# Issuing a chunk's four output blocks in one run on TensorE, with the side work of their positions behind them

## The chip, the cores and the metric

The kernel runs on one core of one Trainium2 chip. The metric is the device time of the whole program in microseconds (us), the median of several runs. The core's engines are named as in the profile: PE is TensorE, which multiplies matrices (PEld is its weight load), DVE is VectorE, ACT is ScalarE, POOL is GpSimd, and SP is the engine whose queue issues the DMAs here.

## The reference, cut to what matters

The input is x of shape (32, 128, 56, 56): 32 images of 128 channels and 3136 pixels ("tokens"). A first stage adds a binarised 3x3 convolution with batch normalisation to x. The second stage treats each pixel as a token of 128 numbers:

```python
t = t + ffn(_ln_t(t))
# inside ffn, for each image x (3136 tokens of 128), H = 512, k = 3136/2, kk = k - 1:
weights = (jnp.einsum('bsd,do->bso', x, wr) + br)[..., 0]      # router
_, idx = jax.lax.top_k(weights, k); sel_idx = idx[:, :kk]
h = jax.nn.gelu(jnp.einsum('bkd,dh->bkh', sel, w1) + b1)       # hidden blocks
y = jnp.einsum('bkh,hd->bkd', h, w2) + b2                      # output blocks
y = y * w_sel[..., None]                                       # gate
processed = zeros.at[batch_idx, sel_idx].set(y); return processed + x
```

The kernel computes h and y for all tokens and multiplies y by a gate that is the router's weight for chosen tokens and zero for the others.

## The kernel before, in words

Phase 1 (the convolution, about the first 530 us) is not touched. Phase 2 is one program for each engine, written out by hand, with semaphores between them. It handles an image in 7 chunks of 448 tokens, and a chunk in 8 positions, so an image has 56 positions (POS). The body `phase2(n, b)` runs over them in order; `c, j = divmod(pos, 8)`.

- At j 0 to 3 PE computes hidden block j of chunk c (three f16 matmuls, L939 to L941) into PSUM bank j; ACT drains it through GELU into `hs` (L495).
- At j 4 to 7 PE computes output block j - 4 of the chunk before (L950, f32, two matmul records for a block). The four blocks accumulate into one PSUM bank, which ACT drains into `yo` (L505, at j 7).
- After the block of a position comes its side work: steps of other images and stages, which tables of positions place (`TRANSPOSE_AT`, `NORM_AT`, and so on; a position from 56 on is in the next image's body). `due` looks up what is due at a position.

The side steps that this document speaks of:

- Token statistics of image n+1: PE transposes a chunk (L885; T0 to T6 at positions 1, 3, 4, 5, 9, 10, 11) into bank BC0 (even chunks) or BC1 (odd), and DVE takes statistics from it (`tile_stats`, L647). From the third on, a transpose waits until DVE has taken the one before the last. DVE turns them into mean and reciprocal deviation (POOL helps, then L670 on DVE), PE transposes these (`rows_of_stats`, L904, position 23), DVE splits them (the last step is L679), and SP copies them into rows with six DMAs (L369).
- Normalisation: `spread_stats` (positions 31, 39, 47, 54, then 7, 15, 20 of the next body) spreads these rows over the partitions, L917 into BC0 and L920 into BC1; DVE multiplies (u, L685) and subtracts (t, L694). L917 waits until transposes' statistics are taken. L920 waits until the gate before it has been used, since both live in BC1.
- Gate: `spread_gates` (positions 19, 24, 29, 33, 38, 45, 52; L930) spreads a chunk's gates into BC1, and DVE multiplies (`apply_gate`, L781).
- Search for the top k: DVE counts (L722), PE sums the counts (`sum_counts`, L959; positions 35, 39, 42, 46, 50, 53, then 2, 5), DVE chooses (L728). Then PE does `transpose_ties` (position 10), `scan_ties` (L972, position 13), and DVE makes the gates from it (L767 to L775); SP copies them to rows with three DMAs. Router matmuls (L895) stand at 15, 16, 17, 20, 21, 23, 27.

DVE walks through the positions in the same order with its own share of these steps, so each engine answers the other in turn. Bodies -1 to 2 and 29 to 32 are written out, bodies 3 to 28 are a hardware loop with two bodies a turn.

Of the kernel before, what the change touches and what calls it, by code (L numbers as in the profile page):

```python
# [21 lines left out]
NCH = TOK // T  # L22
# [6 lines left out]
NB = HID // C  # L29
# [48 lines left out]
def block_kernel(nc, consts, x_in, cw_in, cb_in, gamma_in, beta_in, wr_in, br_in, w1_in, b1_in,  # L78
# [12 lines left out]
    with ExitStack() as ctx:  # L91
# [167 lines left out]
        def wait_count(eng, semaphore, value):  # L259

            if not (isinstance(value, int) and value <= 0):
                eng.wait_ge(semaphore, value)
# [12 lines left out]
        def is_int(n):  # L275
            return isinstance(n, int)

        def has(n, low=0, high=n_img):

            return not is_int(n) or low <= n < high  # L280
# [6 lines left out]
        def due(table, shift, n, b, pos):  # L287

            steps = [table] if is_int(table) else table
            found = []  # L290
            for at, m, mb in ((pos, n + shift, (b + shift) % 2), (pos + POS, n + shift - 1, (b + shift + 1) % 2)):
                if at in steps and has(m):
                    found.append((m, mb, steps.index(at)))
            return found
# [533 lines left out]
        def _(pe):  # L828
# [46 lines left out]
            def transposes(m, b, c, n, pos):  # L875
                pe.wait_ge(x1_ready, m * NCH + c + 1)

                wait_count(pe, t_ready if c % 2 else u_ready, done(NORM_AT, 1, n, pos))
                if c % 2:
                    wait_count(pe, gated, done(OUT_AT, -1, n, pos))  # L880
                if c > 1:
                    pe.wait_ge(stats_taken, m * NCH + c - 1)
                for i in range(TPG):
                    lo = c * T + i * TILE
                    last = nc.tensor.transpose(ps[0:TILE, BC0 + c % 2, i * C:(i + 1) * C], xb[b][:, lo:lo + TILE], ident)  # L885
                last.then_inc(transposed, 1)

            def router(n, b, c):

                pe.wait_ge(tl_ready, n * NCH + c + 1)  # L890
                if c == 0 and has(n - 1):
                    pe.wait_ge(mask_step, (n - 1) * MASK_STEPS + 3)
                bank = ps[:, T_BANK, 0:T]
                for i, (w, t) in enumerate(((wsel_h, th), (wsel_h, tl), (wsel_l, th))):
                    last = M(bank, w[:, C - c:2 * C - c], cut(t, c), start=c == 0 and i == 0,  # L895
                             stop=c == NCH - 1 and i == 2)
                if c == NCH - 1:
                    last.then_inc(w_done, 1)

            def rows_of_stats(m, n, pos):  # L900
                pe.wait_ge(mr_ready, m + 1)
                wait_count(pe, u_ready, done(NORM_AT, 1, n, pos))
                for q in range(2):
                    last = nc.tensor.transpose(ps[0:NT, BC0, q * C:q * C + TILE], rm[:, q, :],  # L904
                                               ident[0:TILE, 0:TILE])
                last.then_inc(stat_rows, 1)

            def spread_stats(m, b, c, n, pos):

                g = m * NCH + c  # L910
                if c == 0:
                    pe.wait_ge(norm_rows_in, (m + 1) * 2 * PIECES * 16)

                wait_count(pe, u_ready, g)
                wait_count(pe, stats_taken, done(TRANSPOSE_AT, 1, n, pos + 1))
                wait_count(pe, rms_ready, done(STAT_AT, 1, n, pos + 1))
                M(ps[:, BC0, 0:T], ones_b[0:PIECES, :], cut(rows[0:PIECES, :], c), start=True, stop=True).then_inc(bc_stats, 1)  # L917
                wait_count(pe, t_ready, g)
                wait_count(pe, gated, done(OUT_AT, -1, n, pos + 1))
                M(ps[:, BC1, 0:T], ones_b[32:32 + PIECES, :], cut(rows[32:32 + PIECES, :], c), start=True, stop=True).then_inc(bc_stats, 1)  # L920

            def spread_gates(m, b, c, n, pos):
                g = m * NCH + c
                if c == 0:
                    pe.wait_ge(gate_rows_in, (m + 1) * PIECES * 16)

                wait_count(pe, gated, g)
                wait_count(pe, t_ready, done(NORM_AT, 1, n, pos))
                wait_count(pe, stats_taken, done(TRANSPOSE_AT, 1, n, pos + 1))
                M(ps[:, BC1, 0:T], ones_b[64:64 + PIECES, :], cut(rows[64:64 + PIECES, :], c), start=True, stop=True).then_inc(bc_gate, 1)  # L930

            def hidden(n, b, c, j):
                g = n * NCH + c
                if j == 0:
                    pe.wait_ge(tl_ready, g + 1)
                wait_count(pe, h_ready, (g - 1) * NB + j + 1)
                bank = ps[:, H_BANK + j, 0:T]
                blk = slice(j * C, (j + 1) * C)
                M(bank, w1_h[:, blk], cut(th, c), start=True, stop=False)  # L939
                M(bank, w1_h[:, blk], cut(tl, c), start=False, stop=False)  # L940
                M(bank, w1_l[:, blk], cut(th, c), start=False, stop=True).then_inc(h_done, 1)  # L941

            def output(n, b, c, j):
                g = n * NCH + c
                if j == 0:
                    wait_count(pe, y_taken, g)
                first, final = j == 0, j == NB - 1
                bank = ps[:, Y_BANK, 0:T]
                pe.wait_ge(h_ready, g * NB + j + 1)
                last = M(bank, w2_c[:, j, :], hs[(b + c) % 2][:, j, :], start=first, stop=final)  # L950
                if j == NB - 1:
                    last.then_inc(y_done, 1)

            def sum_counts(n, r):

                pe.wait_ge(part_counts, n * ROUNDS + r + 1)
                if r == 0:
                    pe.wait_ge(w_taken, n + 1)
                M(cnt_ps, cnt_c[:, :].to_broadcast([C, C]), cand_sel[:, :], start=True,  # L959
                  stop=True).then_inc(counts_summed, 1)  # L960

            def transpose_ties(n):
                pe.wait_ge(ties_ready, n + 1)
                R = slice(0, MR_ROWS)
                nc.tensor.transpose(ps[0:MR_COLS, T_BANK, 0:MR_ROWS], ties_sb, ident[R, R])
                M(off_ps, kt[R, K_ONES:K_ONES + MR_ROWS], rowg_c[R, :], start=True, stop=False)
                M(off_ps, kt[R, K_STRI:K_STRI + MR_ROWS], rowe_c[R, :], start=False, stop=True).then_inc(ties_t, 1)

            def scan_ties(n):

                pe.wait_ge(ties_copied, n + 1)
                M(ps[0:MR_ROWS, T_BANK, C:C + MR_COLS], et[:, :], kt[0:MR_COLS, K_TRIU:K_TRIU + MR_COLS],  # L972
                  start=True, stop=True).then_inc(ties_scanned, 1)

            def phase2(n, b):
                for pos in range(POS):
                    c, j = divmod(pos, 2 * NB)

                    if j < NB and has(n):
                        hidden(n, b, c, j)  # L980
                    if j >= NB and c > 0 and has(n):
                        output(n, b, c - 1, j - NB)
                    if j >= NB and c == 0 and has(n - 1):
                        output(n - 1, 1 - b, NCH - 1, j - NB)

                    at = (n, b, pos)
                    for m, mb, c in due(TRANSPOSE_AT, 1, *at):
                        transposes(m, mb, c, n, pos)
                    for m, mb, c in due(ROUTER_AT, 0, *at):
                        router(m, mb, c)  # L990
                    for m, mb, r in due(COUNT_AT, 0, *at):
                        sum_counts(m, r)
                    for m, mb, _ in due(MASK_AT, 0, *at):
                        transpose_ties(m)
                    for m, mb, _ in due(SCAN_AT, 0, *at):
                        scan_ties(m)
                    for m, mb, _ in due(STAT_AT, 1, *at):
                        rows_of_stats(m, n, pos)
                    for m, mb, c in due(OUT_AT, -1, *at):
                        spread_gates(m, mb, c, n, pos)  # L1000
                    for m, mb, c in due(NORM_AT, 1, *at):
                        spread_stats(m, mb, c, n, pos)

            pairs(pe, phase2, *P2, -1, n_img + 1)


# [20 lines left out]
```

## Time and profile before

| | before |
|---|---|
| time, median of 3 runs | 2380.06 us (2378.2 to 2380.43) |
| time of the profiled execution | 2379.78 us |
| its span | 2377.8 us |
| mean granted TensorE clock | 0.981 of 2.4 GHz |
| PE busy | 2202.0 us, 93% |
| DVE busy | 1622.5 us, 68% |
| ACT busy | 1222.9 us, 51% |
| POOL busy | 918.5 us, 39% |
| output matmuls L950 | 1792 records, 806.9 us, 564 ns each |

The busy shares are of the span. A matmul record overlaps the next one, so the step from one start to the next says more about PE than a record's length.

### The profile page before, as it was taken

To read this page: it belongs to the slowest core of one execution; us is meant where nothing else is said; L and a number is where in the kernel's file an instruction comes from. 1 tells how busy PE (TensorE), PEld (TensorE's weight loads), DVE (VectorE), ACT (ScalarE), POOL (GpSimd) and SP (SyncE) were. 2 spreads that over 40 slices of the span, in tenths; PEclk is the share of its full clock that TensorE was granted. 3 is DMA by queue.
4 is the path that set the end of the run, shared out by engine and by line. 5 is a ranking of instruction groups with operands and counts; after the bars stand their busy time and mean duration, and the time that the engine had idled before them with its cause. 6 is when DMAs were issued, how large, how long until landed. Compare 5 with 4: busy or idle time off the path is not lost. (4 is left out here: it accounts for less than half of the span.)

```text
span 2377.8 us, 38759 instructions
## 1 busy us (share of the span) xinstructions
PE 2202.0 (93%) x9739; PEld 1071.6 (45%) x9739; DVE 1622.5 (68%) x4887; ACT 1222.9 (51%) x2030; POOL 918.5 (39%) x714
## 2 busy tenths in 40 slices
PE   6999999966999999999999999998999999999997
PEld 3555555533444444444444444444444444444443
DVE  6777777755677766767676666666667676767764
ACT  4444444434555555555555555555555555555553
POOL 1000000024455544445445555454544454554433
PEclk9999999987999999999999999999999999999998
DMA  3444444431122222222222222222222222222201
GB/s 146 163 162 162 162 162 162 162 122 46 62 73 73 74 81 76 81 85 75 73 73 73 73 73 72 73 73 73 81 82 91 73 73 73 73 73 84 73 33 59
DMA packets 66710, 216.99 MB, mean 91 GB/s; under 512 B 28496, under 2 KB 33328, under 8 KB 62640
## 3 DMA queue, kind: packets, MB, share of 16 engines
q1 hardware_dynamic: 66464, 215.71, 25.1%
q14 instruction: 84, 0.69, 0.1%
q8 instruction: 18, 0.29, 0.1%
q10 hardware_dynamic: 144, 0.30, 0.0%
HBM read 136.70 MB, written 77.47 MB: 90 GB/s over the span
## 5 line engine op out<-in xcount | busy, mean ns | idle before, releaser
L950 PE MATMUL ps<-hs,w_c 128*128 128x448 f32 x1792 | 806.9, 564 | 0.8 <-ACT yo L505 0.6
L495 ACT ACTIVATE hs<-ps,b1c,undo 128x448 f32<-128x448 f32 x896 | 602.6, 718 | 136.6 <-PE ps L941 136.0
L412 POOL TENSOR_TENSOR tl<-tr,th 128x448 f16<-128x448 f32 x224 | 245.5, 1096 | 515.7 <-ACT th L518 393.9
L854 PE MATMUL ps<-yo,cwT 128*128 128x448 bf16 x2016 | 425.6, 356 | 0.0
L950 PEld LDWEIGHTS ps<-hs,w_c 128*128 128x128 f32 x1792 | 305.3, 192 | 191.7 <-issue 152.3
L505 ACT ACTIVATE yo<-ps,cols 128x448 f32<-128x448 f32 x224 | 141.9, 633 | 453.6 <-PE ps L950 453.6
L407 POOL TENSOR_TENSOR xb<-xb,zr 128x448 f32<-128x448 f32 x224 | 259.1, 1159 | 182.7 <-ACT zr L511 181.8
L419 POOL TENSOR_TENSOR yo<-yo,base 128x448 f32<-128x448 f32 x224 | 264.5, 1181 | 167.4 <-DVE yo L781 166.6
L939 PE MATMUL ps<-th,w_h 128*128 128x448 f16 x896 | 321.4, 359 | 0.0
L941 PE MATMUL ps<-th,w_l 128*128 128x448 f16 x896 | 319.3, 356 | 0.0
L940 PE MATMUL ps<-tl,w_h 128*128 128x448 f16 x896 | 319.2, 356 | 0.0
L854 PEld LDWEIGHTS ps<-yo,cwT 128*128 128x128 bf16 x2016 | 179.2, 98 | 196.2 <-issue 48.7
L476 ACT ACTIVATE y<-ps 128x448 f16<-128x448 f32 x224 | 121.9, 544 | 263.2 <-PE ps L854 263.2
L781 DVE TENSOR_TENSOR yo<-yo,ps 128x448 f32<-128x448 f32 x224 | 138.6, 619 | 152.4 <-PE ps L930 150.7
L647 DVE BATCH_NORM_STATS2 st<-ps 112x6 f32<-112x128 f32 x896 | 192.7, 282 | 62.9 <-PE ps L885 60.5
L511 ACT ACTIVATE zr<-y,bn_t,bn_s 128x448 f32<-128x448 f16 x224 | 168.8, 754 | 122.2 <-DMA y<-y_int 109.6
L685 DVE TENSOR_TENSOR ur<-xb,ps 128x448 f32<-128x448 f32 x224 | 138.5, 618 | 134.8 <-PE ps L917 76.5
L571 DVE BATCH_NORM_STATS2 base<-y 128x448 f16 (+1 forms) x224 | 140.5, 627 | 130.2 <-ACT y L476 130.2
L518 ACT ACTIVATE th<-tr 128x448 f16<-128x448 f32 x224 | 129.3, 577 | 139.8 <-DVE tr L694 127.6
L426 POOL TENSOR_TENSOR rm<-stw,kt 112x28 f32<-112x28 f32 x32 | 153.6, 4799 | 78.8 <-DVE stw L665 78.8
L885 PE MATMUL ps<-kt,xb 128*112 128x128 f32 x896 | 140.4, 281 | 41.7 <-DVE st L647 28.8
L403 POOL TENSOR_TENSOR sm<-sm,kt 128x1 f32<-128x1 f32 x1 | 0.6, 566 | 459.7 <-DVE sm L635 459.7
(131 smaller groups left out, 2709.7 us busy)
## 6 DMA issues: line engine op xcount, KB each, us to landing
xb<-x SPq DMA_DIRECT2D x31, 1568.0 KB, 7.6
xb<-x SPq DMA_DIRECT2D x33, 896.0 KB, 4.7
result<-yo SPq DMA_DIRECT2D x32, 896.0 KB, 4.4
y_int<-y SPq DMA_DIRECT2D x32, 784.0 KB, 3.7
xb<-x SPq DMA_DIRECT2D x33, 672.0 KB, 4.3
result<-yo SPq DMA_DIRECT2D x32, 672.0 KB, 3.4
y<-y_int SPq DMA_DIRECT2D x32, 448.0 KB, 5.3
y<-y_int SPq DMA_DIRECT2D x32, 336.0 KB, 4.8
```

The source lines that it names most:

```text
L407: nc.gpsimd.tensor_tensor(cut(xb[b], c), cut(xb[b], c), zr[(b + c) % 2][:, :], ALU.add).then_inc(x1_ready, 1)
L412: nc.gpsimd.tensor_tensor(cut(tl, c), tr[(b + c) % 2][:, :], cut(th, c), ALU.subtract).then_inc(tl_ready, 1)
L419: nc.gpsimd.tensor_tensor(cut(yo[b], c), cut(yo[b], c), cut(base[b], c), ALU.add).then_inc(out_ready, 1)
L426: nc.gpsimd.tensor_tensor(rm[:, 0, :], stw[:, 5, :], kt[0:TILE, K_MHALF:K_END], ALU.pow).then_inc(rstd_ready, 1)
L495: nc.scalar.activation(hs[(b + slot) % 2][:, j, :], ps[:, H_BANK + j, 0:T], ACT.Gelu_apprx_tanh, bias=b1c[:, j:j + 1], scale=undo[:, 1:2]) ...
L511: nc.scalar.activation(zr[(mb + c) % 2][:, :], cut(y16[mb], c), ACT.Relu, bias=bn_t[:, :], scale=bn_s[:, :]).then_inc(relu_ready, 1)
L647: last = V.bn_stats(st[:, c * TPG + i, :], ps[0:TILE, BC0 + c % 2, i * C:(i + 1) * C])
L854: last = M(bank, cwT[:, t, :], sg[b][:, c * ROWS + dy:c * ROWS + dy + ROWS, dx:dx + SIDE], start=t == 0, stop=t == TAPS - 1)
L939: M(bank, w1_h[:, blk], cut(th, c), start=True, stop=False)
L940: M(bank, w1_h[:, blk], cut(tl, c), start=False, stop=False)
L941: M(bank, w1_l[:, blk], cut(th, c), start=False, stop=True).then_inc(h_done, 1)
L950: last = M(bank, w2_c[:, j, :], hs[(b + c) % 2][:, j, :], start=first, stop=final)
```

## The change

PE's `phase2` no longer issues output block j - 4 at each of the positions j 4 to 7. At j 4 it issues all four, and then the side work of that position; j 5, 6 and 7 hold side work alone. No other engine's program changes, and no instruction is added or removed.

```diff
                     if j < NB and has(n):
                         hidden(n, b, c, j)
-                    if j >= NB and c > 0 and has(n):
-                        output(n, b, c - 1, j - NB)
-                    if j >= NB and c == 0 and has(n - 1):
-                        output(n - 1, 1 - b, NCH - 1, j - NB)
+                    for k in range(NB if j == NB else 0):
+                        if c > 0 and has(n):
+                            output(n, b, c - 1, k)
+                        if c == 0 and has(n - 1):
+                            output(n - 1, 1 - b, NCH - 1, k)
```

On PE, positions 3 to 7 of a body read before the change as follows. L885 are the transposes, L950 an output block, L959 the sum of counts, L917 and L920 the statistics spread at position 7.

```order
L885 MATMUL ps<-kt,xb 112x128 x4
L950 MATMUL ps<-hs,w_c 128x448
L885 MATMUL ps<-kt,xb 112x128 x4
L950 MATMUL ps<-hs,w_c 128x448
L885 MATMUL ps<-kt,xb 112x128 x4
L959 MATMUL ps<-cand_sel,cnt_c 128x15
L950 MATMUL ps<-hs,w_c 128x448 x2
L917 MATMUL ps<-rows,ones_b 128x448
L920 MATMUL ps<-rows,ones_b 128x448
```

The same place after the change:

```order
L885 MATMUL ps<-kt,xb 112x128 x4
L950 MATMUL ps<-hs,w_c 128x448 x4
L885 MATMUL ps<-kt,xb 112x128 x8
L959 MATMUL ps<-cand_sel,cnt_c 128x15
L917 MATMUL ps<-rows,ones_b 128x448
L920 MATMUL ps<-rows,ones_b 128x448
```

Transposes T2 and T3 now follow each other, and nothing stands between them, the sum and L917.

On PE, positions 35 to 39 (L930 is the gate spread of position 38) before:

```order
L959 MATMUL ps<-cand_sel,cnt_c 128x15
L950 MATMUL ps<-hs,w_c 128x448 x3
L930 MATMUL ps<-rows,ones_b 128x448
L950 MATMUL ps<-hs,w_c 128x448
L959 MATMUL ps<-cand_sel,cnt_c 128x15
L917 MATMUL ps<-rows,ones_b 128x448
L920 MATMUL ps<-rows,ones_b 128x448
```

and after:

```order
L959 MATMUL ps<-cand_sel,cnt_c 128x15
L950 MATMUL ps<-hs,w_c 128x448 x4
L930 MATMUL ps<-rows,ones_b 128x448
L959 MATMUL ps<-cand_sel,cnt_c 128x15
L917 MATMUL ps<-rows,ones_b 128x448
L920 MATMUL ps<-rows,ones_b 128x448
```

The output block that stood between L930 and L920 now stands ahead of L930. Positions 45 to 47 and 52 to 54 change in the same way. At positions 12 to 15 the scan L972, which stood after two of four output blocks, now stands after all four, directly ahead of the router matmuls L895:

```order
L950 MATMUL ps<-hs,w_c 128x448 x4
L972 MATMUL ps<-kt,et 98x32
L895 MATMUL ps<-th,wsel_h 128x448
L895 MATMUL ps<-tl,wsel_h 128x448
L895 MATMUL ps<-th,wsel_l 128x448
L917 MATMUL ps<-rows,ones_b 128x448
L920 MATMUL ps<-rows,ones_b 128x448
```

## Rows read from the trace of the kernel before

**Rows 1.** Timeline, positions 12 to 19: start us, us, engine, line, operation [idle before]
```profile
1697.71 1.67 PE L950 MATMUL ps<-hs,w_c 128*128 128x448 f32 x4
...
1699.31 0.35 PE L972 MATMUL ps<-kt,et 32*98 32x32 f32 x2
...
1699.70 0.25 DVE L767 TENSOR_SCALAR mk<-ps,srch 98x32 f32<-98x32 f32 x1 [0.28 <-PE ps L972]
...
1705.86 0.34 PE L930 MATMUL ps<-rows,ones_b 3*128 3x448 bf16 x1
```

**Rows 2.** Timeline of the same image, positions 20 to 23
```profile
1707.65 0.36 PE L917 MATMUL ps<-rows,ones_b 3*128 3x448 bf16 x1
...
1709.29 0.49 DVE L670 SCALAR_TENSOR_TENSOR rm<-stw,rm 112x28 f32<-112x28 f32 x1
...
1711.44 0.36 PE L904 MATMUL ps<-kt,rm 112*28 112x112 f32 x2
```

**Rows 3.** Timeline of the image before, positions 23 to 31
```profile
1656.22 0.36 PE L904 MATMUL ps<-kt,rm 112*28 112x112 f32 x2
...
1664.42 0.36 PE L917 MATMUL ps<-rows,ones_b 3*128 3x448 bf16 x1 [1.11 <-DMA rows<-rms]
```

**Rows 4.** Timeline, positions 36 to 39
```profile
1669.04 2.49 PE L950 MATMUL ps<-hs,w_c 128*128 128x448 f32 x6
1671.47 0.36 PE L930 MATMUL ps<-rows,ones_b 3*128 3x448 bf16 x1
...
1672.72 0.36 PE L920 MATMUL ps<-rows,ones_b 3*128 3x448 bf16 x1
```

**Rows 5.** Timeline of DVE beside them
```profile
1671.86 0.62 DVE L781 TENSOR_TENSOR yo<-yo,ps 128x448 f32<-128x448 f32 x1 [0.93 <-PE ps L930]
```

**Rows 6.** Timeline, positions 44 to 47
```profile
1675.55 1.68 PE L950 MATMUL ps<-hs,w_c 128*128 128x448 f32 x4
...
1679.26 0.36 PE L920 MATMUL ps<-rows,ones_b 3*128 3x448 bf16 x1
```

**Rows 7.** Timeline, position 52 to position 4 of the next body, no loop turn
```profile
1681.86 0.92 PE L950 MATMUL ps<-hs,w_c 128*128 128x448 f32 x2
...
1682.71 0.36 PE L930 MATMUL ps<-rows,ones_b 3*128 3x448 bf16 x1
...
1685.49 0.61 DVE L685 TENSOR_TENSOR ur<-xb,ps 128x448 f32<-128x448 f32 x1
...
1687.09 0.60 PE L885 MATMUL ps<-kt,xb 128*112 128x128 f32 x4
...
1687.73 0.89 DVE L647 BATCH_NORM_STATS2 st<-ps 112x6 f32<-112x128 f32 x4 [0.56 <-PE ps L885]
...
1689.13 0.92 PE L950 MATMUL ps<-hs,w_c 128*128 128x448 f32 x2
```

**Rows 8.** Timeline, positions 4 to 9 of that body
```profile
1692.08 0.89 DVE L647 BATCH_NORM_STATS2 st<-ps 112x6 f32<-112x128 f32 x4
...
1693.45 0.36 PE L917 MATMUL ps<-rows,ones_b 3*128 3x448 bf16 x1
...
1694.08 0.61 DVE L685 TENSOR_TENSOR ur<-xb,ps 128x448 f32<-128x448 f32 x1
...
1694.89 0.60 PE L885 MATMUL ps<-kt,xb 128*112 128x128 f32 x4
```

**Rows 9.** Timeline, positions 1 to 9 of a body that follows a loop turn
```profile
1632.24 0.89 DVE L647 BATCH_NORM_STATS2 st<-ps 112x6 f32<-112x128 f32 x4 [3.27 <-PE ps L885]
...
1638.81 0.61 DVE L685 TENSOR_TENSOR ur<-xb,ps 128x448 f32<-128x448 f32 x1
...
1639.52 0.60 PE L885 MATMUL ps<-kt,xb 128*112 128x128 f32 x4
```

**Rows 10.** Timeline of PE after another loop turn, position 5
```profile
1521.58 1.07 PE L885 MATMUL ps<-kt,xb 128*112 128x128 f32 x4 [1.26 <-DVE st L647]
```

**Rows 11.** That stretch: busy PE, PEld, DVE, ACT, POOL; granted clock; DMA share, GB/s
```profile
1521.00:1523.00 2.00, 1.42 (x6) 1.39 (x7) 1.50 (x10) 0.00 (x0) 0.00 (x0) 0.59 0.80 240
```

## The prediction

> **What bounds the kernel now.** I read the busy shares first (PE 93%), then the waits, and then the timeline of two images on all engines, row by row, because a reordering can only be priced at the places where one engine waits for another. The reader is to see in the rows how PE and DVE answer each other in turn. PE is nearly always the later of the two: it has work left when DVE's answer comes. Its few waits are short: 1.11 us at position 31 for the six DMAs of the statistics rows [rows 3], and after a loop turn two waits for DVE, the second 1.26 us [rows 10]. DVE starts a loop turn 3.27 us late [rows 9]; the row names PE, but T0 was done long before, so this is the turn of DVE's own program. What makes PE's waits so short is the output block, 0.75 us long (two blocks take 1.60 us up to the next side step [rows 1] and one takes 0.85 [rows 7]), that lies between a question to DVE and the next PE step that needs the answer. The change takes these blocks out from between.
>
> **The change, part by part.** Nothing is added or removed, so every cost is a wait. Times are offsets within one image. The delay from a DVE end to the PE start it releases is 0.1 us: u ends at 1639.42 and T4 starts at 1639.52 [rows 9]. I use it throughout.
>
> A. Positions 12 to 19. The scan L972 starts 1.60 us after the first output block [rows 1]; with four blocks ahead of it, 1.60 + 2 x 0.75 = 3.10, so 1.50 later. DVE builds the gates from it (L767 starts 0.39 after L972), SP copies them to rows, and L930 at position 19 needs them: 1705.86 - 1699.70 = 6.16 us after L767 [rows 1]. Between lie three DMAs that SP issues behind the gates, and no work that could be pulled closer. The row of L930 shows no wait, so PE and the rows come at about the same time today; I take it that L930 moves by the whole 1.50. Were the rows early by some tenths, the term would be so much less; by its nearest rows it lies between 1.0 and 1.5 and can't be below, since the rows come 1.50 later in any case. The router matmuls at position 15 wait for L767 too, but that hides under the same 1.50. **+1.50.**
>
> B. Positions 20 to 23. L930 to L917 is 1.79 us with one output block between [rows 1, 2]; with four, 1.79 + 2.25 = 4.04. L917 to the end of L670 on DVE is 1709.78 - 1707.65 = 2.13, and L904 needs L670. Before, three output blocks stood between and L904 came at 5.58 after L930. Now L904 comes at 4.04 + 2.13 + 0.10 = 6.27. **+0.69.** The wait of 1.11 us behind it [rows 3] doesn't absorb this or A: its chain (DVE's split, six DMAs of SP) starts from L904 itself and moves with it, 8.20 us long as before.
>
> C. Positions 36 to 39. Three blocks and L930: 2.43 us; with four, 3.18 [rows 4]. L920 writes the bank that the gate product L781 reads. L781 starts 0.39 after L930 and takes 0.62 [rows 4, 5]; before, the fourth block covered that. Now L920 starts at 3.18 + 0.39 + 0.62 + 0.10 = 4.29 instead of 3.68: +0.61. Behind it, L920 to the next output block was 2.83 us against 2.60 one chunk later [rows 4, 6, 7], since the sum at position 42 waited for a count; DVE now starts that count earlier against PE, which gives 0.23 back. **+0.38.**
>
> D. Positions 44 to 47, the same: 3.10 + 1.11 = 4.21 against 3.71 [rows 6]. **+0.50.**
>
> E. Position 52 to 9 of the next body. L930 moves from 0.85 to 3.10 after the first block [rows 7]. All that DVE does from here to the chunk's u (L685) hangs on L930 in a fixed order: u ends 3.39 after L930. T0 needs u, because both use BC0. So T0 starts at 3.10 + 3.39 + 0.10 = 6.59 instead of 5.23. The first block of position 4 comes 2.04 later [rows 7], at 8.63. T2, before one block behind, now stands four blocks behind: 11.64. DVE starts its statistics 0.64 after a transpose [rows 7], so T2's run from 12.28 to 13.17, T3's from 13.27 (0.1 for the choose between). L917 at position 7 needs T3's statistics: 13.27 + 0.89 + 0.10 = 14.26 instead of 11.59. DVE's next u starts 2.00 after the start of T3's statistics [rows 8], at 15.27, ends at 15.88, and T4 follows at 15.98 instead of 13.03. **+2.95.**
>
> E after a loop turn. Here DVE is already the one that is waited for: T4 starts as soon as u ends [rows 9]. DVE's whole sequence from L930 through the turn moves with L930, by 3.10 - 0.85. **+2.25.**
>
> The counts come from the code. A and B occur in 31 bodies, C and D in 30. E occurs in 30, of which 12 follow a jump back of the loop (13 turns, bodies 3 to 28). Sum: 31 x 1.50 = 46.5; 31 x 0.69 = 21.4; 30 x 0.88 = 26.4; 18 x 2.95 + 12 x 2.25 = 80.1. Together 174 us. The savings of unsplit runs are inside: a switch between an output block and a three-row matmul costs 0.1 us (0.85 against 0.75), and each term is a difference of starts that contains it.
>
> The clock. After the two waits behind a loop turn the granted clock fell to the lower level, 1.2 GHz: it averages 0.59 over 1521 to 1523, and T3's four matmuls took 1.07 us instead of 0.60 [rows 8, 10, 11]. With the change PE works little between T2 and T4 after a turn. T2 starts at the earliest when T0's statistics are taken, 0.89 + 0.10 after their start, and T4 starts 1639.52 - 1632.24 = 7.28 after it [rows 9]. In these 6.3 us PE now has two transpose groups, a sum, L917 and L920 and two hidden blocks, and no output block: I estimate under 2.5 us of work. I count a fall in each of the 12. Its price lies between 0.5 us (the one transpose group) and 1.6 us (two such stretches of 2 us at 0.59); I take 1.2, as the PE work right behind it is dense but partly covered by waits. That is 14 us. The Trainium skill, "TensorE: Matmul & The Clock Gate", section "HAM oscillation — how this bites in real kernels", says that an engine which idles between bursts is put back to half rate; this trace agrees at 0.59. By its rule the falls come wherever waits pile up, which is the third rival below.
>
> Sum: 174 + 14 = 188 us on the profiled execution's own 2379.78 us (span 2377.8, and 2 us around it), which is within 0.3 us of the median of the runs. That gives 2568 us.
>
> **The rivals.**
>
> 1. Faster: PE is 93% busy, and what counts is its switches. About 12 splits an image go, at 0.1 us each, 1.2 x 31 = 37 us: 2343. For it speaks the switch cost in the rows. It decides if DVE's answer comes before PE asks for it. Against it: between L930 and L920 must lie 1.1 us of PE work (0.39 + 0.62 + 0.10), and after the change there is one 15-column sum and L917, some 0.3 us. The Trainium skill, same page, section "Loop structure matters more than you think", recommends just this form, the matmuls of one output tile back to back with the drain behind them; its rule would give this rival's sign, while in these rows the matmuls between are what hides DVE. Chance 0.03.
>
> 2. Half of E doesn't come. If DVE catches up in the long run of output blocks of position 4 (it has 3 us there), so that only T0's delay of 1.36 us stays, E is 30 x 1.36 = 41 instead of 80, and with no fall of the clock the time is 2380 + 94 + 41 = 2515. For it speaks that DVE is busy only 68%. Against it speaks its fixed order: T2's statistics can't start before T2. Chance 0.13.
>
> 3. The clock falls oftener. The waits of A (1.3 us), B, C and E come in images without a loop turn as well; one more fall in each of 31 images at up to 1.6 us adds 50: 2618. For it speaks that the two waits before the fall in the rows are no longer than these. Against it: the waits of A, B and C stand apart, with a run of four output blocks (3 us) or hidden blocks between them. Chance 0.20.
>
> 4. No change: what sets the pace is the row DMAs of position 31, and delays ahead of them are absorbed: 2380. Against it: their chain starts from L904, which is itself delayed. Chance 0.02.
>
> My forecast has 0.62.
>
> **How the numbers follow.** The time is the forecast's, 2568. The range reaches from rival 2 to a little above rival 3: 2510 to 2628. It holds the forecast (its own range is 2540 to 2600) and most of rivals 2 and 3. A difference under 0.2% can't be told from none in this kernel, as its runs spread by 0.1%. Faster 0.03 (rival 1), same 0.02 (rival 4), slower 0.95.
>
> **What would show it.** In the profile after: L972 3.1 us after the first block of position 12, and a wait of over 1 us for the gate rows at position 19 (A); L904 waiting for DVE L670 (B); L920 waiting for DVE L781, some 0.8 us, three times an image (C, D, E); T0 waiting for u and L917 at position 7 for DVE L647, 1.5 us or more (E); the period of an image near 61 us without a loop turn. The prediction is wrong if L917 or L920 start without a wait, if L930 at position 19 stays put against position 12, or if the granted clock of phase 2 drops far below 0.95, which would put it too low.

## The result and the profile after

| | before | after |
|---|---|---|
| time, median of 4 runs each | 2380.0 us (2378.2 to 2380.43) | 2617.06 us (2616.24 to 2617.91) |
| ratio | 1 | 1.0998, 95% interval 1.0979 to 1.1017 |
| span of the profiled execution | 2377.8 us | 2615.5 us |
| mean granted TensorE clock | 0.981 | 0.944 |
| period of an image without loop turn or clock fall (after: one such image) | 55.4 us | 61.8 us |

The change costs 237 us, 10%. It is slower, as forecast, and inside the range, but 49 us above the predicted 2568. The page of the kernel after, with its busy shares and the row of the granted clock over 40 slices:

```profile
span 2615.5 us, 38759 instructions
PE 2294.0 (88%) x9739; PEld 1131.5 (43%) x9739; DVE 1618.6 (62%) x4887; ACT 1220.0 (47%) x2030; POOL 926.5 (35%) x714
PEclk9999999978999898999999999998999999989998
```

The work is the same (9739, 4887, 2030 and 714 instructions), DVE, ACT and POOL are busy as long as before, and PE 92 us longer for the same matmuls. The rest of the 237 us is idle time. PE's waits in the kernel after (line waited at, what for: us in total, times, longest):

```profile
PE ps L917 <- DMA rows<-rms: 75.8, 32, 7.9
PE ps L917 <- issue: 41.2, 31, 1.5
PE ps L930 <- DMA rows<-mks: 36.4, 32, 5.7
PE ps L920 <- DVE yo L781: 33.6, 90, 0.4
...
PE ps L904 <- DVE rm L670: 16.4, 32, 8.5
```

L920 waits for the gate product L781 ninety times, 30 images by three. Before, it waited for L781 nowhere, and 0.5 us in all for L694. "L917 <- issue" (31 times 1.3) is the wait at position 7: the profile finds no releaser, but each time DVE's statistics L647 end just ahead.

The rows that answer to [rows 1, 2, 4, 6 to 8], timeline of PE in the kernel after (start, us, operation, idle before), from position 44 to position 23 of the next body:

```profile
1697.42 3.17 PE L950 MATMUL ps<-hs,w_c 128*128 128x448 f32 x8
1700.52 0.36 PE L930 MATMUL ps<-rows,ones_b 3*128 3x448 bf16 x1
...
1701.60 0.36 PE L920 MATMUL ps<-rows,ones_b 3*128 3x448 bf16 x1 [0.31 <-DVE yo L781]
...
1706.06 3.17 PE L950 MATMUL ps<-hs,w_c 128*128 128x448 f32 x8
1709.06 1.04 PE L885 MATMUL ps<-kt,xb 128*112 128x128 f32 x8
...
1711.58 0.34 PE L917 MATMUL ps<-rows,ones_b 3*128 3x448 bf16 x1 [1.47 <-issue]
...
1713.26 0.65 PE L885 MATMUL ps<-kt,xb 128*112 128x128 f32 x4
...
1716.12 3.17 PE L950 MATMUL ps<-hs,w_c 128*128 128x448 f32 x8
1719.22 0.35 PE L972 MATMUL ps<-kt,et 32*98 32x32 f32 x2
...
1725.52 0.34 PE L930 MATMUL ps<-rows,ones_b 3*128 3x448 bf16 x1 [1.05 <-DMA rows<-mks]
...
1729.57 0.36 PE L917 MATMUL ps<-rows,ones_b 3*128 3x448 bf16 x1
...
1731.45 0.36 PE L904 MATMUL ps<-kt,rm 112*28 112x112 f32 x2 [0.28 <-DVE rm L670]
```

Read it stretch by stretch against the same stretch before. Position 12 to 19, from L950 to L930, is 9.40 us (1725.52 - 1716.12) instead of 8.15. Positions 19 to 23 take 5.93 (1731.45 - 1725.52) instead of 5.58. L917 at position 7 comes 5.52 after the first block (1711.58 - 1706.06), and T4 1.68 behind it.

From here on, a fall is a stretch in which the granted clock drops to 1.2 GHz. I took the same differences of PE starts in every image. The first columns of the table are medians of the images without loop turn and without a fall in the stretch. In the kernel after, only 3 of 29 images are without a fall in C, but the experiment without falls further down has the same 6.85. The last two are sums of after minus before over the 29 images that lie whole in the traces: all of it, and the part of it that is also there in an experiment further down, in which nearly all falls are gone.

| stretch | before, us | after, us | forecast | measured | sum, 29 images | of it at the full clock |
|---|---|---|---|---|---|---|
| A: block at 12 to L930 at 19 | 8.14 | 9.38 | +1.50 | +1.24 | 34.7 | 35.0 |
| B: L930 at 19 to L904 | 5.58 | 5.93 | +0.69 | +0.35 | 9.4 | 9.5 |
| L904 to L917 at 31 | 8.19 | 9.07 | 0 | +0.88 | 25.6 | 25.7 |
| L917 at 31 to position 36 | 4.74 | 4.8 | 0 | +0.1 | 8.5 | -0.7 |
| C: 36 to 44 | 6.51 | 6.85 | +0.38 | +0.34 | 36.6 | 10.2 |
| D: 44 to 52 | 6.30 | 6.85 | +0.50 | +0.55 | 15.3 | 15.3 |
| E: 52 to position 12 | 15.85 | 18.70 | +2.95 | +2.85 | 99.1 | 80.7 |
| sum | | | | | 229.3 | 175.7 |

So 229 of the 237 us lie in these 29 images: 176 in waits, and 53 go with the clock. The kernel before has a few falls of its own, so this split is good to a few us. Two things stand out. A stretch that the change doesn't touch grew by 0.88 us (L904 to position 31); and C costs 36.6 us where 29 x 0.34 would be 10. The first is a slower instruction on DVE, the second the clock.

**The slower instruction.** Timeline of all engines in the kernel after, at DVE's last split step of the statistics rows, L679:

```profile
1731.98 1.04 POOL L412 TENSOR_TENSOR tl<-tr,th 128x448 f16<-128x448 f32 x1 [1.48 <-ACT th L518]
...
1732.98 1.17 POOL L407 TENSOR_TENSOR xb<-xb,zr 128x448 f32<-128x448 f32 x1
...
1733.18 1.21 DVE L679 TENSOR_TENSOR rms<-rrest,rms 28x224 bf16<-28x224 f32 x1
...
1734.41 4.84 SPq L369 DMA_DIRECT2D rows<-rms  x6
...
1740.51 0.36 PE L917 MATMUL ps<-rows,ones_b 3*128 3x448 bf16 x1 [2.17 <-DMA rows<-rms]
```

L679 takes 1.21 us and ends 0.24 after POOL's L407 (1734.39 against 1734.15). In the kernel before the two stood apart:

```profile
1711.78 1.14 POOL L407 TENSOR_TENSOR xb<-xb,zr 128x448 f32<-128x448 f32 x1
...
1713.07 0.38 DVE L679 TENSOR_TENSOR rms<-rrest,rms 28x224 bf16<-28x224 f32 x1
```

All executions of L679, first before, then after (count: shortest/median/longest in ns, first and last start in us, form):

```profile
L679 DVE TENSOR_TENSOR rms<-rrest,rms x32: 378/379/380, 539.3 to 2278.0; 28x224 bf16<-28x224 f32 x32
```
```profile
L679 DVE TENSOR_TENSOR rms<-rrest,rms x32: 378/1205/1210, 538.7 to 2510.0; 28x224 bf16<-28x224 f32 x32
```

PSUM is the memory into which PE writes its results here, SBUF the one in which the other operands lie. L679 has both inputs in SBUF. The first two DVE steps of the same split, L676 and L677, read PSUM and keep their 0.38 us in all 32 executions. (The third, L678, a cast out of SBUF, varies in both kernels, from 0.26 to 0.64 us.) So an instruction of DVE with both inputs in SBUF is held up beside POOL's addition: L679 lost 0.83 us of the 0.97 for which the two overlapped.

The change also took two such instructions out from beside POOL, and these became shorter. L670 took 0.49 us beside L407 before [rows 2] and takes 0.18 now, with POOL idle beside it (the last line of the rows after). L769, the second step of the gates in A, stood beside L407 before:

```profile
1699.24 1.13 POOL L407 TENSOR_TENSOR xb<-xb,zr 128x448 f32<-128x448 f32 x1 [0.64 <-ACT zr L511]
...
1699.99 0.42 DVE L769 TENSOR_TENSOR mk<-mk 98x32 f32<-98x32 f32 x1
...
1701.77 2.51 SPq L363 DMA_DIRECT2D rows<-mks  x3
```

and after:

```profile
1719.90 0.19 DVE L769 TENSOR_TENSOR mk<-mk 98x32 f32<-98x32 f32 x1
...
1721.45 2.51 SPq L363 DMA_DIRECT2D rows<-mks  x3
...
1731.21 0.18 DVE L670 SCALAR_TENSOR_TENSOR rm<-stw,rm 112x28 f32<-112x28 f32 x1
```

All executions of L769, before and after:

```profile
L769 DVE TENSOR_TENSOR mk<-mk x32: 191/432/630, 623.9 to 2359.0; 98x32 f32<-98x32 f32 x32
```
```profile
L769 DVE TENSOR_TENSOR mk<-mk x32: 191/192/193, 626.2 to 2596.7; 98x32 f32<-98x32 f32 x32
```

L930 starts 4.09 us after the first of the three DMAs is issued before (1705.86 - 1701.77) and 4.07 after (1725.52 - 1721.45), so the gate rows set its start in both kernels. What became shorter is the way from the scan L972 to L930, 6.30 us (1725.52 - 1719.22) for 6.55 (1705.86 - 1699.31), nearly all of it L769's 0.23.

The Trainium skill, "SBUF — State Buffer", section "Who interferes with whom", says that a DVE instruction with two SBUF inputs contends with a GpSimd instruction that reads SBUF, over a port pair that is an exclusive lock, and that one with at most one SBUF input, outside the 2-port modes, does not. This trace agrees, at 1.21 against 0.38 us for L679 and 0.38 throughout for L676 and L677.

**The clock.** Behind the wait at position 31, windows of the kernel after (us, busy us and instructions of PE, PEld, DVE, ACT, POOL, then granted clock, DMA share, GB/s):

```profile
1740.00:1743.00 3.00, 2.18 (x10) 0.80 (x11) 1.24 (x2) 1.20 (x2) 0.21 (x1) 0.84 0.12 31
1743.00:1746.00 3.00, 2.97 (x9) 1.27 (x9) 1.88 (x6) 2.01 (x4) 2.12 (x2) 0.50 0.92 296
1746.00:1749.00 3.00, 3.00 (x5) 1.33 (x4) 1.12 (x4) 0.56 (x2) 0.00 (x0) 0.52 0.94 384
1749.00:1752.00 3.00, 2.60 (x9) 0.86 (x8) 1.24 (x5) 1.63 (x3) 1.31 (x2) 1.00 0.04 14
```

and the output blocks of position 36 among them:

```profile
1745.52 4.91 PE L950 MATMUL ps<-hs,w_c 128*128 128x448 f32 x8
```

PE is idle 2.17 us, is then busy for 1.7 us (the spread and two hidden blocks), and from about 1742.1 on it runs at 0.50, the level of 1.2 GHz, through the hidden blocks of position 34 and into the four output blocks: 4.91 us for what takes 3.17 at the full clock. A fall between positions 31 and 44 is there in 4 of the 29 images before, and in 26 after. Behind a loop turn, between T2 and position 12, there is one in 3 of 12 images before and in 10 after. One such image, windows around T3 to T4 (T3 starts at 1775.13, T4 at 1779.71):

```profile
1774.00:1776.00 2.00, 0.63 (x5) 0.48 (x5) 1.95 (x13) 0.00 (x0) 0.00 (x0) 1.00 0.55 125
1776.00:1778.00 2.00, 1.09 (x4) 0.48 (x5) 1.80 (x11) 0.00 (x0) 0.00 (x0) 0.55 0.97 400
1778.00:1780.00 2.00, 2.00 (x8) 0.96 (x6) 1.25 (x4) 1.17 (x3) 0.00 (x0) 0.50 0.40 163
```

In the images with a fall there, E takes 23.25 us, in the two without 20.58: 2.7 us a fall. Summed over the 29 images, 24 us before and 225 us after are spent at the lower level.

### The profile page after: what moved, and what is told of

Same layout as the page of the kernel before. It is cut to its first block and busy times, and to the rows that moved or that the text cites. A ratio compares the mean times of both kernels' runs of the same rounds, so it can differ in the third digit from the quotient of the medians.

```text
span 2615.5 us, 38759 instructions
## 1 busy us (share of the span) xinstructions
PE 2294.0 (88%) x9739; PEld 1131.5 (43%) x9739; DVE 1618.6 (62%) x4887; ACT 1220.0 (47%) x2030; POOL 926.5 (35%) x714
## 5 line engine op out<-in xcount | busy, mean ns | idle before, releaser
L950 PE MATMUL ps<-hs,w_c 128*128 128x448 f32 x1792 | 745.9, 560 | 0.0
L950 PEld LDWEIGHTS ps<-hs,w_c 128*128 128x128 f32 x1792 | 344.7, 199 | 283.6 <-issue 236.2
L412 POOL TENSOR_TENSOR tl<-tr,th 128x448 f16<-128x448 f32 x224 | 254.4, 1136 | 599.9 <-ACT th L518 590.2
L781 DVE TENSOR_TENSOR yo<-yo,ps 128x448 f32<-128x448 f32 x224 | 138.6, 619 | 368.0 <-PE ps L930 367.9
L939 PE MATMUL ps<-th,w_h 128*128 128x448 f16 x896 | 340.1, 380 | 4.1 <-issue 4.0
L941 PE MATMUL ps<-th,w_l 128*128 128x448 f16 x896 | 339.4, 379 | 0.0
L940 PE MATMUL ps<-tl,w_h 128*128 128x448 f16 x896 | 339.2, 379 | 0.0
L407 POOL TENSOR_TENSOR xb<-xb,zr 128x448 f32<-128x448 f32 x224 | 255.4, 1142 | 218.4 <-ACT zr L511 217.6
L647 DVE BATCH_NORM_STATS2 st<-ps 112x6 f32<-112x128 f32 x896 | 194.2, 281 | 84.6 <-PE ps L885 44.1
L885 PE MATMUL ps<-kt,xb 128*112 128x128 f32 x896 | 146.4, 294 | 53.5 <-DVE st L647 23.6
L917 PE MATMUL ps<-rows,ones_b 3*128 3x448 bf16 x224 | 83.5, 373 | 119.8 <-DMA rows<-rms 75.8
```

The source lines that it names most:

```text
L407: nc.gpsimd.tensor_tensor(cut(xb[b], c), cut(xb[b], c), zr[(b + c) % 2][:, :], ALU.add).then_inc(x1_ready, 1)
L412: nc.gpsimd.tensor_tensor(cut(tl, c), tr[(b + c) % 2][:, :], cut(th, c), ALU.subtract).then_inc(tl_ready, 1)
L647: last = V.bn_stats(st[:, c * TPG + i, :], ps[0:TILE, BC0 + c % 2, i * C:(i + 1) * C])
```

## The experiments

Times and ratios are against the kernel before on the same chip: 2377.24 us for the pieces `(1,)`, `(2,)`, `(4, 5)` and `(6, 0)`, 2378.43 for the last experiment, 2379.29 for the others. Stretches of 29 images are taken in the profiled executions.

### One chunk in a run at a time

One edit, with another set in each kernel, writes the run of four for some chunks and leaves the rest as before:

```diff
-                    if c > 0 and j >= NB and has(n):
-                        output(n, b, c - 1, j - NB)
+                    for k in (range(NB) if j == NB else ()) if c in (1,) else (j - NB,) if j >= NB else ():
+                        if c > 0 and has(n):
+                            output(n, b, c - 1, k)
```

(and the same for c = 0). `(1,)` is term A alone:

> Only the output blocks of positions 12 to 15 are issued in one run (term A alone); all other chunks stay split as before. My theory: the scan moves 1.5 us later and L930 at position 19 some 1.2 us, nothing behind it takes that up: 31 x 1.2 = 37 us, 2417 us, ratio 1.016. Rival: the wait of 1.1 us for the row DMAs at position 31 takes it up: ratio 1.000.

Measured 2413.28 us, 1.0154 (1.0134 to 1.0174), clock 0.983. That is 36 us, 1.16 for each of 31 images, near the 1.20 that the table gives on average (34.7 us in 29 images). The rival, that the wait for the row DMAs at position 31 takes it up, is out.

`(2,)`, term B alone:

> Only positions 20 to 23 in one run (term B alone). In the whole change L904 came 0.33 us later against L930, and the way from L904 to L917 at position 31 was 0.88 us longer than before. If the 0.88 belong to this edit itself: 31 x 1.2 = 37 us, 2417 us. If they come from where GpSimd's additions happen to lie against DVE's last split step, they depend on the delays of the other edits too, and this kernel may show 0.33 alone: 10 us, 2390 us, ratio 1.004.

Measured 2420.06 us, 1.0179 (1.0155 to 1.0202), clock 0.971. 43 us is more than B's 0.35 x 31 = 11. All executions of L679 in this kernel:

```profile
L679 DVE TENSOR_TENSOR rms<-rrest,rms x32: 378/1205/1208, 539.0 to 2317.9; 28x224 bf16<-28x224 f32 x32
```

The slow split step comes with the run of positions 20 to 23 alone: that moves L904, and so L679, into POOL's work. It brings 26 us (30 x 0.88). With B's 11 that is 37 of the 43. The 6 left go with the clock (0.971 against 0.981): there is a fall between positions 31 and 44 in 16 of 29 images instead of 4, and these stretches take 8 us more.

`(4, 5)`, terms C and D:

> Only positions 36 to 39 and 44 to 47 in one run (terms C and D alone). My theory: L920 waits for the gate product on DVE in both, and the clock doesn't fall, since the two waits are 0.4 us each: 30 x 0.85 = 26 us, 2406 us, ratio 1.011. Rival: in the whole change position 36 to 39 cost 1.2 to 1.8 us, not 0.6; if that is a wait and not the clock, this kernel shows it too: 30 x 2 = 60 us, 2440 us.

Measured 2411.1 us, 1.0146 (1.0125 to 1.0166), clock 0.980: 34 us where 26 were forecast, and not the 60 of the rival. Over the 29 images C and D take 28.5 us more, near the forecast. Most of the rest is E with 8 us more: there is a fall behind 8 of 12 loop turns instead of 3, so the clock did fall oftener, though not behind the two waits in question.

`(6, 0)`, term E:

> Only positions 52 to 55 and 4 to 7 in one run (term E alone). My theory: 2.87 us in each of 18 images without a loop turn and 2.26 in 12 with one, 79 us; and after a loop turn the granted clock falls, some 2 us each, 25 us: 2485 us, ratio 1.044. Rival: half of it is taken up by DVE, so that only T0's 1.33 us stay: 40 us, 2420 us.

Measured 2476.64 us, 1.0431 (1.0407 to 1.0456), clock 0.973: 99 us, between the prediction's 94 (80 and the 14 of the clock) and the 104 expected just above, and not the 41 of the rival in which DVE catches up. Over the 29 images E takes 90 us more, and no other stretch changes by more than 2.

`(3,)`, positions 28 to 31, which the forecast priced at nothing:

> Only positions 28 to 31 in one run, the one place to which my prediction gave no cost. PE waits for the row DMAs at position 31 either way: ratio 1.000, within 0.002. If the gate product that now comes later held up L920 or anything behind it, up to 0.7 us an image: 2400 us.

Measured 2378.81 us, 1.0004 (0.9992 to 1.0017): nothing, as forecast. PE waits for the rows at position 31 either way, 1.30 us now and 1.10 before. That these blocks cover nothing doesn't follow: the wait for the rows would hide it, and the last experiment shows that it does. The clock is a little lower too, 0.974 in the profiled execution, with a fall between positions 31 and 44 in 11 of 29 images instead of 4.

The four costly pieces make 36 + 43 + 34 + 99 = 212 us; the whole makes 237. The 25 us more go with the clock: in the profiled executions no piece alone brings it below 0.971, the whole brings it to 0.944. Over the 29 images the whole exceeds the four pieces together by 35 us, and 29 of these lie between positions 31 and 44.

### Filling the waits with matmuls that nobody needs

To see what the clock costs, PE got work to do in the longest waits: 10 extra bf16 matmuls ahead of the statistics spread at position 31, 6 at position 7, 9 at position 5 of every second body. They write a free PSUM bank and read what is there anyway; no result uses them.

```diff
+FILL = {31: 10, 7: 6}
...
+            def fill(n, c, count):
+                g = n * NCH + c
+                wait_count(pe, h_ready, g * NB + 1)
+                for _ in range(count):
+                    M(ps[:, H_BANK, 0:T], ones_b[:, :], cwT[:, 0:4, :].rearrange("p t i -> p (t i)")[:, 0:T],
+                      start=True, stop=True)
```

> The whole change, and in addition matmuls whose result nobody reads, placed where PE waits: 10 at position 31 ahead of L917, 6 at position 7 ahead of L917, and 9 at position 5 ahead of T3 in odd images (the ones after a loop turn). They take at most what the wait lasts (0.19 us each), so the waits stay. Theory (the part of the loss that the moved waits don't explain is the granted clock, which falls after them): the falls go, some 50 us come back, 2565 us, ratio 1.078; up to 5 us of that are lost in odd images outside the loop. Rival (it is further waits): 2617 us or more.

Measured 2570.77 us, 1.0802 (1.0784 to 1.0821), clock 0.985. Timeline of this kernel at position 31 (L980 are the extra matmuls, L918 is L917, L951 is L950):

```profile
1711.11 2.06 PE L980 MATMUL ps<-cwT,ones_b 128*128 128x448 bf16 x10
1713.37 0.36 PE L918 MATMUL ps<-rows,ones_b 3*128 3x448 bf16 x1 [0.20 <-DMA rows<-rms]
...
1718.01 3.25 PE L951 MATMUL ps<-hs,w_c 128*128 128x448 f32 x8
```

The spread still waits for its rows, but PE does not idle, and the four blocks of position 36 take 3.25 us, not 4.91. PE has 656 instructions more and the kernel is 46 us shorter. A fall between positions 31 and 44 is left in 1 of 29 images, none behind a loop turn, and one in E in 4 images without a turn. The rival, further waits, is out. So the falls cost at least 2617.1 - 2570.8 = 46 us of the time after, a fifth of the loss; the other 191 us at most are waits at the full clock. Over the 29 images the sums differ by 53.5 us, in just the three stretches where the falls were: 9.2 from position 31 to 36, 26.4 in C and 18.4 in E, and nothing elsewhere (A, B and D stay within 0.3). The last column of the table above is this kernel minus the kernel before.

### Moving POOL's work away from the slow split step

One entry of a table puts the work of a chunk of the image after next (ACT's relu, POOL's addition L407) at position 26 instead of 22, in the kernel with the change:

```diff
-RELU_AT = [9, 14, 18, 22, 37, 39, 45]
+RELU_AT = [9, 14, 18, 26, 37, 39, 45]
```

> The whole change, with one entry of a table moved: the residual of chunk 3 (ReLU on ScalarE and its addition on GpSimd) at position 26 instead of 22. Theory: GpSimd's addition holds up DVE's L679 (1.21 us instead of 0.38); without it L904 to L917 at position 31 falls back from 9.06 to 8.2 us: 26 us less than the whole change, 2591 us. Rival: the way is longer because of ScalarE or the DMA queue: 9.06 us stay, 2617 us.

Measured 2565.08 us, 1.0776 (1.0751 to 1.0801), clock 0.961. All executions of L679 in it:

```profile
L679 DVE TENSOR_TENSOR rms<-rrest,rms x32: 378/380/381, 540.3 to 2458.9; 28x224 bf16<-28x224 f32 x32
```

L679 is back at 0.38 in all 32, and the way from L904 to position 31 at 8.24 us, so the rival (ACT or the queue) is out. This gives 52 us, twice the 26 that I had expected. Over the 29 images, against the kernel after, the stretch from L904 to position 31 gives 24.0 of it; 6.7 come between position 31 and 36 and 25.3 in C, where the falls are: 15 images have one instead of 26. E takes 4.7 us more, with a fall in 9 images without a loop turn instead of 1.

All kernels of this document together show how these falls go with the wait at position 31 (its median, and the images of 29 with a fall between positions 31 and 44; the last two kernels are those of the next section):

| kernel | wait, us | images with a fall |
|---|---|---|
| two queues; with the run on top | 0; 0.07 | 0; 0 |
| whole change with filled waits | 0.18 | 1 |
| `(6, 0)`; `(4, 5)`; `(1,)`; before | 1.07; 1.09; 1.10; 1.10 | 2; 4; 0; 4 |
| `(3,)`; whole change with POOL's work moved | 1.30; 1.35 | 11; 15 |
| `(2,)`; whole change | 1.98; 2.17 | 16; 26 |

A longer wait goes with more falls. That the wait alone decides isn't shown: what PE does around it differs from kernel to kernel too.

### Two queues for the statistics rows

The wait at position 31 is there before the change too (1.11 us, [rows 3]). SP issues six small DMAs one after the other, 4.84 us. Here ACT issues three of them; the rest is the kernel before:

```diff
-                    for q in range(2):
+                    for q in range(1):
...
+                    if pos == 25 and has(n + 1):
+                        act.wait_ge(rms_ready, n + 2)
+                        for s in range(PIECES):
+                            act.dma_start(rows[32 + s:33 + s, :].rearrange("a (j p) -> a j p", p=TILE),
+                                          rms[:, s, 1, :]).then_inc(norm_rows_in, 16)
```

> The kernel before, split blocks, with one thing moved: three of the six row DMAs of the token statistics are issued by ScalarE at position 25 instead of by SP. SP issues six in 4.84 us; with three it is done 2.4 us earlier, and PE's waits at position 31 (1.1 us) and 35 (0.9 us) hang on it. Theory: both waits go, up to 2 us in each of 31 images, 62 us: 2318 us, ratio 0.974. Rival: ScalarE's queue is held up by the wait and the issues, and hidden blocks wait for GELU: 2380 us or more.

Measured 2306.72 us, 0.9694 (0.9678 to 0.971), clock 0.986: 3.1% faster than the kernel before, and the best of all kernels here. Timeline of the two queues in it:

```profile
1661.92 2.45 SPq L369 DMA_DIRECT2D rows<-rms  x3
1661.93 2.37 ACTq L510 DMA_DIRECT2D rows<-rms  x3
```

PE's waits for the rows and for the counts in this kernel (lines moved by 5):

```profile
PE ps L922 <- DMA rows<-rms: 5.8, 1, 5.8
...
PE ps L964 <- DVE junk L727: 3.2, 5, 2.1
```

and in the kernel before:

```profile
PE ps L917 <- DMA rows<-rms: 43.1, 32, 7.9
...
PE ps L959 <- DVE junk L722: 24.1, 24, 1.3
```

Not only the wait for the rows is gone (43.1 to 5.8), but also that for the counts, which stood behind it (24.1 to 3.2). I had counted on the first alone; 37 + 21 = 58 of the 73 us are these two; its list of waits for other things is nearly unchanged, and the other 15 us I can't place by it (the clock is a little higher, 0.986 for 0.981). The differences of starts place most: over the 29 images the way from L904 to position 36 is 62 us shorter, and C 3, where the kernel before had falls and this one has none. The rival, that ACT's queue is held up, is out.

The same with the whole change on top:

> The kernel of act_rows (three of the six row DMAs issued by ScalarE) with the four output blocks of each chunk in one run. Theory: the terms A to E stay, since none of them waits for these DMAs; the fall of the clock that followed the wait of 2.2 us at position 31 mostly goes with that wait. So the run costs less than the 237 us that it cost without the move, 180 to 200 us: 2307 + 190 = 2497 us. Rival (the two add up): 2307 + 237 = 2544 us.

Measured 2502.63 us, 1.0511 (1.0491 to 1.0531), clock 0.974. The run of four costs 2502.6 - 2306.7 = 196 us here and 237 without the second queue. The 41 us between them are what the run loses less when the wait at position 31 has been taken away first; the rival, that the two add up, is out. By stretches over the 29 images, the run costs 192 us here and 229 without the second queue. From L904 to position 31 it costs nothing, where it cost 26, though L679 still takes 1.21 us: PE now comes there no earlier than the rows. C costs 11 instead of 37, with no fall between positions 31 and 44. But from position 31 to 36 it costs 26 us instead of 9, and this is a term that the prediction had put at nothing, the run of positions 28 to 31. With the wait for the rows gone, L920 (here L925) waits at position 31 for the gate product too, 0.31 us in the median, and the sum of counts behind it waits again. PE's waits in this kernel:

```profile
PE ps L925 <- DVE yo L786: 43.4, 119, 0.8
```

These are 119 waits instead of the 90 of the kernel after.

## Why the prediction was right, and where it was off

**The mechanism was right.** PE and DVE answer each other in turn, and the output block between question and answer is what hid DVE. All signs but two came as stated: L972 is 3.10 us after the first block (1719.22 - 1716.12), L930 at position 19 waits 1.05 for the gate rows, L904 waits for L670, L920 waits for L781, and L917 at position 7 waits behind L647. That last wait was to be 1.5 us or more; it is 1.47 in the image shown and 1.33 on average. The idle of L920 is 0.31 to 0.4 us instead of some 0.8: the 0.8 was the distance from L917, and L917 and the sum lie in it. The period without loop turn is 61.8 us, forecast 61, and the granted clock of phase 2 (from 552 us on) is 0.94.

**A, 1.50, measured 1.24.** The row of L930 showed no wait, and I took it that PE and the gate rows come at about the same time and L930 moves by all of 1.50. The first is so: the rows set L930's start in both kernels. What I had wrong is the chain from the scan to the rows, which I carried over as it was. L769 in it had stood beside POOL's addition (0.42 us, in other images up to 0.63) and takes 0.19 now. On average A costs 1.20, so it is 31 x 0.3 = 9 us less.

**B, 0.69, measured 0.35.** L930 to L917 came as computed (4.05 against 4.04). What followed was shorter: I carried L670's row of 0.49 over [rows 2], and it takes 0.18 once POOL's addition no longer lies beside it. 10 us less.

**The stretch from L904 to position 31, 0, measured 0.88.** This is the step that failed. I wrote that its chain "moves with it, 8.20 us long as before". It moved, but L679 in it came to lie beside POOL's work and took 1.21 us for 0.38. 26 us more, shown by the edit of one table entry and by the run of positions 20 to 23 alone. It is the same step as in A and B: a duration of DVE was carried over without a look at POOL beside it. There this made the term too high, here it left one out.

**C, D and E** came within 0.1 us a piece (0.34, 0.55, 2.85 for 0.38, 0.50, 2.95), and E behind a loop turn at 2.25 for 2.25 (18.33 to 20.58, images without a fall).

**The clock, 14, measured 46 to 53.** This is the larger miss. I counted a fall in each of 12 images, at 1.2 us. The kernel before already pays 1.6 for one there (19.91 against 18.33 us for E). Behind the turns they came in 10, at 2.7 us, since a fall lasts into the next stretch of dense work; and 22 more images than before have one behind position 31, worth 36 us (9.2 + 26.4), which I had counted at nothing. That is rival 3 in its mechanism, one more fall an image. Its text named the waits of A, B, C and E; what brought the falls was E's, as forecast, and the wait of position 31, twice as long as before (2.17 us for 1.11) with short steps behind it. Against rival 3 I had written that runs of four blocks stand between the waits. There they don't: one run is ahead of the wait, at position 28, and the next at 36.

The forecast's waits were 174 us; measured are 176 in 29 images, or about 188 for all 31 (two more at 6.1). They were near partly by luck: A and B were too high by some 20, and the instruction on DVE was missing with 26. The total of 2617 agrees with rival 3's 2618, but with 14 us more in waits, and as much less in the clock, than that sum has.

Rival 1 (the switches count, faster) has nothing to show: DVE's answer came late at each of its places. Rival 2 (DVE catches up) fell with the run of positions 52 and 4 alone, 99 us. Rival 4 fell with A alone, 36 us.

## What to carry to other kernels

When PE and another engine answer each other in turn, the independent matmuls between are cover, and to bundle them uncovers each answer; price it place by place as the difference of two starts, which here came within 0.1 us where no neighbour changed. Before carrying a duration over, look at what lies beside it on POOL, and at what it will lie beside once it has moved: the same instruction took 0.38 or 1.21 us, and the three waits that were mispriced by more than 0.1 us (A, B and the way from L904 to position 31) come from this. A cost that is hidden behind a wait comes back when the wait is taken away. A wait of 2 us on PE costs more than itself where the clock falls behind it, and splitting a queue that issues six small DMAs in a row gained 3.1% here, where the order of the matmuls gained nothing.

## What the runs showed of the hardware that was not expected

- A DVE instruction of 28 x 224 elements with both inputs in SBUF takes 0.38 us alone and 1.21 beside POOL's, ending 0.24 after it; two of the same size that read PSUM take 0.38 in all 32 executions.
- TensorE, busy 88% of the span, lost at least 46 us of 2617 to the clock behind waits of 1 to 2.2 us. 656 matmuls that nobody needs, put into them, gave these 46 us back (clock 0.985 for 0.944). With a wait of 1.35 us instead of 2.17 at one place, 15 of 29 images had a fall behind it instead of 26.
- The six DMAs of the rows take 4.84 us on one queue, 2.4 us on two, though each moves only 6.1 KB: the time lies in the issuing.
